# The last attention tile's sum and its two halves are made in the next program block

## What is computed

```python
x = x + layernorm(attention(layernorm(x)))
x = x + layernorm(moe(layernorm(x)))
# attention, per batch of 1024 rows
q, k, v = split(x @ w_qkv.T)
out = softmax(q @ k.T / 4) @ v            # (1024, 256)
out = swapaxes(out).reshape(...) @ w_proj.T + b_proj
# moe: 16 experts over all 8192 rows, each takes its 1024 best rows
scores = softmax(x @ gate_w.T); topk per expert
eo = (gelu(xg @ Wg.T) * (xg @ Wu.T)) @ Wd.T * weight   # hidden width 1024
out = scatter_add(eo) + shared expert (the same, hidden width 512, all rows)
```

## Time and profile before

| | us |
|---|---|
| median of 3 runs (lowest 1979.83, highest 1982.16) | 1981.45 |
| the profiled execution, device time | 1987.56 |
| its span, first to last instruction | 1985.7 |
| PE busy in it | 1954.9 |
| DVE busy | 1365.0 |
| ACT busy | 1036.0 |
| POOL busy | 522.6 |

### The profile page before, as it was taken

How to read it: one execution, slowest core, us unless ns; L and a number is a source line. 1 busy time by engine, 2 the same in 40 slices (tenths; PEclk the granted TensorE clock), 3 DMA queues, 4 the chain that set the end, 5 groups by cost and what they waited for, 6 DMA issues and landing times.

```text
span 1985.7 us, 29127 instructions
## 1 busy us (share of the span) xinstructions
PE 1954.9 (98%) x10638; PEld 1660.2 (84%) x10638; DVE 1365.0 (69%) x2602; ACT 1036.0 (52%) x1929; POOL 522.6 (26%) x626
## 2 busy tenths in 40 slices
PE   8999999999999999899999999999999999999997
PEld 7888888888888888788888888888888888888886
DVE  6777787778776877667676766657565656666647
ACT  5456575666654434445454444545454555445446
POOL 0032032123120001223431432343233323332246
PEclk9999999999999999999999999999999999999999
DMA  3113224243243111343434434343434344434566
GB/s 128 54 33 108 75 98 130 73 116 96 80 165 117 57 64 54 112 84 88 103 83 105 82 97 91 87 105 87 104 92 103 83 108 94 100 80 95 156 219 171
DMA packets 153338, 197.38 MB, mean 99 GB/s; under 512 B 104448, under 2 KB 121088, under 8 KB 145152
## 3 DMA queue, kind: packets, MB, share of 16 engines
q1 hardware_dynamic: 127824, 158.00, 25.4%
q0 software_dynamic: 25392, 37.77, 11.8%
HBM read 114.38 MB, written 59.34 MB: 87 GB/s over the span
## 4 chain that ended last, share of the span: by engine, by line
PE 66%; DVE 2%; POOL 1%; issue 1%; ACT 0%; DMA 0%; DVEq 0%; another core or an unknown queue 0%; SPq 0%; ACTq 0%; POOLq 0%
PE mo_psD L1622 12%; PE mo_psG L60 7%; PE mo_psU L60 7%; PE mo_psG L62 7%; PE mo_psG L61 7%; PE mo_psU L62 7%; PE mo_psU L61 7%; PE mo_psD L1624 6%; PE mo_psD L60 1%; PE mo_psD L62 1%; PE mo_psD L61 1%; PE mo_psX L1347 1%; DVE mo_F L1936 1%; DVE mo_HF L1952 0%; POOL mo_H_lo L2264 0%
## 5 line engine op out<-in xcount | busy, mean ns | idle before, releaser
L1748 ACT ACTIVATE mo_HF<-mo_psG 128x512 f32<-128x512 f32 x320 | 191.2, 598 | 412.3 <-PE mo_psU L62 312.7
L1952 DVE TENSOR_TENSOR mo_HF<-mo_psU,mo_HF 128x512 f32<-128x512 f32 x320 | 220.4, 689 | 224.7 <-ACT mo_HF L1748 216.9
L2246 POOL DMA_INDIRECT ACC<-OUT,mo_GI x128 | 201.7, 1576 | 645.3 <-DVE OUT L2038 633.6
L1622 PE MATMUL mo_psD<-wd,mo_H_hi 128*128 128x512 f32 x1024 | 360.8, 393 | 0.2 <-DVE OUT L2038 0.2
L1624 PE MATMUL mo_psD<-wd,mo_H_lo 128*128 128x256 f32 x1024 | 289.3, 283 | 0.0
L60 PE MATMUL mo_psG<-mo_XT_hi,wg_hi 128*128 128x512 f32 x640 | 256.3, 401 | 3.7 <-DVE mo_XT_lo L1860 1.9
L60 PE MATMUL mo_psU<-mo_XT_hi,wu_hi 128*128 128x512 f32 x640 | 254.0, 397 | 0.0
L62 PE MATMUL mo_psU<-mo_XT_hi,wu_lo 128*128 128x512 f32 x640 | 253.0, 395 | 0.0
L62 PE MATMUL mo_psG<-mo_XT_hi,wg_lo 128*128 128x512 f32 x640 | 252.9, 395 | 0.0
L61 PE MATMUL mo_psU<-mo_XT_lo,wu_hi 128*128 128x512 f32 x640 | 252.8, 395 | 0.0
L61 PE MATMUL mo_psG<-mo_XT_lo,wg_hi 128*128 128x512 f32 x640 | 252.6, 395 | 0.0
(11 more groups left out here) (354 smaller groups left out, 4160.0 us busy)
## 6 DMA issues: line engine op xcount, KB each, us to landing
X1a<-wg_in SPq DMA_DIRECT2D x16, 1024.0 KB
X1a<-wu_in SPq DMA_DIRECT2D x16, 1024.0 KB, 4.8
X1a<-wd_in SPq DMA_DIRECT2D x16, 1024.0 KB, 4.8
XN<-XG SPq DMA_DIRECT2D x8, 1088.0 KB, 4.2
X<-x_in SPq DMA_DIRECT2D x8, 1024.0 KB, 5.4
out_dram<-X SPq DMA_DIRECT2D x8, 1024.0 KB, 6.4
XN2T<-xn2T SPq DMA_DIRECT2D x8, 1024.0 KB, 5.1
X1a<-xt_in SPq DMA_DIRECT2D x7, 1024.0 KB
```

The source lines that it names most:

```text
L1622: pe.matmul(psD[:, t % 2, :], h_hi, wd_both[:, it, :, :].rearrange("p z d -> p (z d)"), start=(it == 0), stop=False)
L1748: a.activation(HF[:, it % 2, :], psG[:, it % 2, :], ACT.Gelu).then_inc(s_gelu, 1)
L1952: v.tensor_tensor(HF[:, it % 2, :], psU[:, it % 2, :], HF[:, it % 2, :], ALU.mult).then_inc(s_mul, 1)
L2246: g.indirect_dma_start(out=io["ACC"], out_offset=bass.IndirectOffsetOnAxis(ap=GI[n % 2][:, 4 * tb + t:4 * tb + t + 1], axis=0), in_=OUT[:, ...
```

## The change

The output of tile 7 of the last round is no longer made in the attention block. The pipeline of the last round has ten steps on ACT and DVE instead of eleven. The three instructions move into the MoE block: the sum becomes the first instruction of DVE's list there (`v_sum`), the high half the first of ACT's (`a_out`), and the low half (`v_out`) stands on DVE's list after the gate's shift. PE waits for the low half (`s_olo`) before projection group k = 1, the first that reads tile 7.

For this, the two output banks of the attention become one PSUM tensor `psOL`, made outside of both blocks, and the MoE block uses it as its `mo_psD`. The buffer `rinv` also moves out of the attention. `Osum` for the last tile is a part of the buffer `Y` that the projection's bias writes later. Three semaphores of the tail are shared with the new steps, so that some waits count one higher (`s_sm`, `s_sme`, `s_yb`).

```diff
-        psO = ctx.enter_context(nc.psum_tensor("psO", [P, 512], F32))
-        psL = ctx.enter_context(nc.psum_tensor("psL", [P, 512], F32))
+        psO, psL = c.psOL[:, 0, :], c.psOL[:, 1, :]
...
-                for step in range(NT + 3):
+                for step in range(NT + 3 if R.ln_next else NT + 2):
...
+        self.s_osum, self.s_ohi, self.s_olo = self.s_sm, self.s_sme, self.s_yb
+        self.Osum, self.last = self.Y[:, NT - 1, :], psD[:, 1, :]
...
         for k in range(4):
             hm, jp = k // 2, k % 2
+            if k == 1:
+                pe.wait_ge(self.s_olo, 1)
...
+    def a_out(self, a):
+        a.wait_ge(self.s_osum, 1)
+        a.activation(self.c.O[0][:, NT - 1, :], self.Osum, ACT.Copy, scale=self.c.rinv[:, NT - 1:NT]).then_inc(self.s_ohi, 1)
+
     def a_exp(self, a, n):
-        a.wait_ge(self.s_sm, n + 1)
+        a.wait_ge(self.s_sm, n + 2)
...
+    def v_sum(self, v):
+        v.tensor_reduce(self.Osum, self.last.rearrange("p (z d) -> p d z", z=2), AX.X, ALU.add).then_inc(self.s_osum, 1)
+
+    def v_out(self, v):
+        v.wait_ge(self.s_ohi, 1)
+        v.scalar_tensor_tensor(self.c.O[1][:, NT - 1, :], self.Osum, self.c.rinv[:, NT - 1:NT], self.c.O[0][:, NT - 1, :].bitcast(F32),
+                               ALU.mult, ALU.subtract).then_inc(self.s_olo, 1)
...
-        v.wait_ge(self.s_sme, n + 1)
+        v.wait_ge(self.s_sme, n + 2)
...
-        psG, psU, psX, psD = (ctx.enter_context(nc.psum_tensor("mo_" + n, [P, 2, 512], F32)) for n in ("psG", "psU", "psX", "psD"))
+        psG, psU, psX = (ctx.enter_context(nc.psum_tensor("mo_" + n, [P, 2, 512], F32)) for n in ("psG", "psU", "psX"))
+        psD = c.psOL
...
-                    pe.wait_ge(tail.s_yb, 4)
+                    pe.wait_ge(tail.s_yb, 5)
...
+            tail.a_out(a)
             tail.a_exp(a, 0)
...
+            tail.v_sum(v)
             tail.v_shift(v, 0)
+            tail.v_out(v)
...
+        c.rinv = mem.new("rinv", [P, NT])
+        c.psOL = ctx.enter_context(nc.psum_tensor("psOL", [P, 2, 512], F32))
```

More of the change, by code:

```diff
@@ L247, in attention @@
         halves, turned = c.halves, c.turned
-        negmax, rowsum, rinv = sb("negmax", [P, NT]), sb("rowsum", [P, NT]), sb("rinv", [P, NT])
+        negmax, rowsum, rinv = sb("negmax", [P, NT]), sb("rowsum", [P, NT]), c.rinv
         st = [sb(f"st{n}", [P, NT, 6]) for n in range(3)]
```

## The result

The kernel with the change took 1984.25 us (median of 20 runs, 1981.78 to 1986.42), the kernel before on the same chip 1981.07 (20 runs, 1979.15 to 1982.49). The ratio is 1.0016, 95% interval 1.0010 to 1.0022: about 3.2 us slower where 3.4 us faster was forecast, and 2.8 us above the upper end of the range.

The account below looks back on a forecast made before the run. PE, busy 98% of the span, was taken as the bound. Meeting 1.79 plus clock 1.59 gave 3.38 us off the median 1981.45: 1978.1 us, chance 0.50, own range 1976.6 to 1979.4, with rivals 1976.3 to 1981.5.

Parts of the forecast that it names:

- The meeting: At the attention block's end, PE would be last to arrive instead of DVE and load weights 1.79 us earlier.
- The clock: In the transposes and projection after the attention block, the clock would stay up instead of falling, saving 1.59 us.
- The new wait: PE's wait for tile 7's low half before the second projection group would cost nothing, with 1.3 us to spare.
- the queues behind the moved work: On ACT and DVE in the MoE block, later work would come earlier, DVE by 2.24 us; no loss booked.
- the third step: In the shared expert, DVE's first product would precede PE's need by 0.34 us instead of 1.26; nothing booked.
- Behind the seam PE works without a pause, so the gain is carried to the end one to one.: After the attention-to-MoE transition, the full 3.38 us saved there would reach the kernel's end, with nothing new on PE.
- The rivals: Meeting's gain alone, 1979.7 (chance 0.29); little gain, 1981.4 (0.07); more than the sum, 1977.0 (0.10); slower, 1983.1 or more (0.04).
- The slower rival: DVE late for the shared expert's third step, at L1570: 1983.1 us with two delays, 1984.9 with three; chance 0.04.
- the two signs of being wrong: The meeting with PE last takes over 1 us, or the gain is lost to a clock falling elsewhere.
- The base: Terms from a profiled execution of 1987.56 us, 6.1 above the median, were taken unscaled from the median 1981.45.

Follow-up runs that it names:

- e7: Kernel before with 32 unused bytes ahead of all tensors, so weights and moving operands shift together; one execution, no time given, pitch of 512-column expert matmuls 232.41 ns.
- e8: Kernel before with 32 unused bytes between XT and HF, moving HF, H and all behind them; one execution, no time given, up pitch (matmuls with wg, wu) 232.9 ns.
- e4: The kernel before, unchanged, timed and profiled once more: ratio 1.0004 (0.9995 to 1.0013).
- e5: Kernel before with one unused tensor of 32 bytes per partition ahead of gw, weights wg, wu, wd staying: 1989.67 us beside 1984.86, ratio 1.0023.
- e9: Kernel before with XT 32 bytes further and HF, H and all behind them 64; one execution, no time given, up pitch (matmuls with wg, wu) 234.25 ns.
- e1: Changed kernel with both placements as before, psOL in PSUM banks 6 and 7, rinv at SBUF's far end: 1981.53 us beside 1984.21 of before, ratio 0.9987.
- e3: Changed kernel with only the SBUF addresses as before (rinv at the far end), PSUM banks as changed: 1982.46 us, ratio 0.9987 to before.
- e2: Changed kernel with only the PSUM banks as before (psOL in 6 and 7), rinv still ahead of gw: 1986.5 us, ratio 1.0014 to before.
- e6: Changed kernel with rinv made 64 bytes long instead of 32, moving everything behind it by 64: 1983.28 us, ratio 0.9995 to before.

## Why the prediction was wrong

**The meeting.** Right. From the start of the attention's last matmul to the first transpose it is 0.61 us (565.02 to 565.63) instead of 2.46: 1.85 gained, 1.79 forecast. With PE as the last engine the meeting is as short as with DVE: 0.30 us from PE's last end (565.30) to its first weight load (565.60).

**The clock.** Right in direction, too large in size. The seam took 11.5 us where the clock fell and 9.84 where it did not, a difference of 1.66 for a term of 1.59. But with the old order the clock fell in three of six profiled executions (before, e7, e8; not in e4, e5, e9), with the new one in none of eight. So an estimate of the term is 0.8 on average, half of 1.66, and of the whole seam 1.85 + 0.8 = 2.7 us; six executions are few for such a share. e1 measured 2.7 (0.8 to 4.4), which does not tell it from the full 3.4. The prediction noted that a timed run need not have paid the fall, and booked it in full all the same. What the Trainium skill, "TensorE: Matmul & The Clock Gate", "Part 4: PE-mode transpose", says of transposes, that the full clock does not engage for them, is not what these runs show: 16 transposes in a row ran at a clock of 1.00 in all eight executions with the new order.

**The new wait, the queues behind the moved work, the third step.** Right: no wait of PE at the second projection group. DVE started the input's low half at 569.71 (forecast 569.66) and the first product at 577.38 (577.42). The cover at the third step was 0.6 instead of 0.34, since PE came to it at 578.62 instead of 578.45.

**"Behind the seam PE works without a pause, so the gain is carried to the end one to one."** This is the step that failed. PE does work without a pause, but the step takes it for granted that its instructions keep their durations. The prediction costed what the change does with instructions and waits, and nothing of where it puts data. The two lines that move `rinv` and `psOL` out of the blocks were not given a cost at all, nor bounds. `psOL`'s was indeed nothing that can be told from noise (e3). `rinv`'s was 4.6 us (e5), or 5.0 between e1 and e2. The sum with it: -2.7 + 4.6 to 5.0 = 1.9 to 2.3; measured were 2.3 in e2 (1.0 to 4.6 by the interval) and 3.2 (2.0 to 4.4) for the change.

**The rivals.** None was this one. The slower rival had its place at the third step, where nothing happened. All four, and the forecast, lay within the 11 us of the seam. Neither of the two signs of being wrong that the prediction named came: the meeting took 0.3 us, and the profile after has no fall of the clock that the one before lacks.

**The base.** The prediction read its terms from an execution that was 6.1 us above the median and said so, but booked its fall of the clock in full. Of its three low stretches of the clock before the end, only the one after 615 us was in all six executions with the old order; that at the seam and that around 800 us were in three each.

**What stays open.** Why the distance matters. The runs show that it does, that it isn't a start on 32 or 64 bytes of one operand (e6, e7), that the two down matmuls mostly move against each other (with 128 bytes the first is 5.4 ns slower, the second 3.3 faster; with 96 both are faster), and that tensors which the matmul doesn't read have a part (e8, e9). Which of the streams from SBUF get in each other's way was not tried. The pitches over the whole kernel, 3840 x 1.75 + 1024 x (1.7 - 2.2) = 6.2 us, are more than the 4.6 to 5.0 measured. From the 4721st matmul on they do add up: between e4 and e5 the distances under 300 ns grow by 5.5 us at the up matmuls and by 1.7 - 2.2 at the down pair, together 5.0, and the rest grew by 5.0 (1163.8 to 1168.8). The difference lies ahead of it, in its 600 up matmuls and their neighbours, where the waits and the low stretches of the clock vary. Whether other distances do better than 128 bytes, or one for XT and another for H, was not tried.

## What to carry to other kernels

Where the bound engine is busy all the time, a change has two kinds of cost: what it does to the order of work, and what its allocations do to the addresses of everything behind them; look for the second in the diff as well, and put a new small buffer where it moves nothing. An even drift between two traces, the same matmuls a little longer all the way, is the sign of it, and an unused tensor in the old kernel is the test. Before a fall of the clock is booked as a gain, look at more than one execution.

## What was not expected of the hardware

The pitch of a 128x512 matmul that follows its weight load depends on where its moving operand and the tensors behind it lie in SBUF against the weights and the others that stay: 232.4 ns at the old distance, 234.2 with 32 bytes more, 233.35 with 64, 233.3 with 96, 227.5 with 128. In the down pair the first went from 230.6 to 232.3, 231.4, 228.7 and 236.0 ns, and the second from 120.2 to 117.9, 119.0, 118.3 and 116.8. Moving all tensors together by 32 bytes changed none of these by more than 0.03 ns. The Trainium skill, "SBUF — State Buffer", "Operand start alignment", says that an operand may start at any multiple of its element size and that this is about legality and not about speed; these runs give the speed: 96 unused bytes were worth 0.8% of the kernel (ratio 1.0016 without them, 0.9933 with them).

An idle time of PE of 2.2 us at the same place was followed by a fall of the clock to 1.2 GHz in three of six executions; one of 0.3 us in none of eight.
